# Four graph layers on one core: the attention blocks' biases added off TensorE, the first block's entry reordered, three buffers for the last mixing sets, the block loop written out

## The reference

```
h = relu(layernorm(x)); x = x + L0(h)    # 2 x [A_norm @ h @ W_gcn + b; leaky_relu(h @ W_mlp + b)]
h = relu(layernorm(x)); x = x + L1(h)    # 4 blocks, see below
h = relu(layernorm(x)); x = x + L2(h)    # h = x @ W + b, 3 diffusion steps with a 0/1 adjacency
h = relu(layernorm(x)); x = x + L3(h)    # 2 relational layers; w[r] = sum_b att[r, b] * basis[b]
```

```
y = cond_layer_norm(x, cond, s1, b1)
q, k, v = y @ wq + bq, y @ wk + bk, y @ wv + bv       # 4 heads of 128
x = x + (segment_softmax(q[src] . k[dst]) @ v) @ wo + bo
y = cond_layer_norm(x, cond, s2, b2)
x = x + relu(y @ m_w1 + m_b1) @ m_w2 + m_b2
```

## Time and profile before

| | |
|---|---|
| median of 3 runs | 886.33 us |
| profiled execution | 891.0 us, span 889.3 us |
| TensorE busy | 839.7 us, 94% |
| VectorE busy | 560.2 us, 63% |
| ScalarE busy | 398.0 us, 45% |
| GpSimd busy | 231.4 us, 26% |
| mean granted clock of TensorE | 0.985 |

### The profile page before, as it was taken

The page is one execution under the profiler, slowest core; times in us unless marked ns, Lnnn a source line. Parts: engine busy times, 40 slices in busy tenths (PEclk is TensorE's granted clock), DMA queues, the critical chain, the costliest instruction groups (busy, mean ns, idle before and its releaser), DMA issues. The chain is left out here.

```text
span 889.3 us, 13979 instructions
## 1 busy us (share of the span) xinstructions
PE 839.7 (94%) x4222; PEld 636.4 (72%) x4223; DVE 560.2 (63%) x1221; ACT 398.0 (45%) x646; POOL 231.4 (26%) x253
## 2 busy tenths in 40 slices
PE   4999789999889999999997999999999998999998
PEld 2666557667677778777695777787786965688786
DVE  5999987748957666576656476664776664730110
ACT  3999893325345612355322365223563233531210
POOL 5000023207422124402235122234013414412200
PEclk9999999999999999999999999999999998999999
DMA  7999914715525653636541546436477377220100
GB/s 167 192 214 241 275 39 124 188 58 133 154 59 123 179 125 107 147 102 178 122 136 54 140 98 183 100 106 146 102 193 176 115 192 184 56 96 0 48 13 35
DMA packets 37846, 113.39 MB, mean 128 GB/s; under 512 B 5908, under 2 KB 6472, under 8 KB 30108
## 3 DMA queue, kind: packets, MB, share of 16 engines
q1 hardware_dynamic: 20604, 79.00, 37.5%
q10 hardware_dynamic: 17184, 33.69, 11.3%
HBM read 105.33 MB, written 7.34 MB: 127 GB/s over the span
## 5 line engine op out<-in xcount | busy, mean ns | idle before, releaser
L690 POOL TENSOR_TENSOR wl<-wraw,wh 128x512 fp32r<-128x512 f32 x140 | 179.7, 1318 | 395.3 <-ACT wh L768 361.7
L1806 PE MATMUL ring<-ohs,ohd 128*128 128x512 f32 x312 | 80.2, 410 | 6.4 <-DVE ohs L1317 6.4
L1806 PEld LDWEIGHTS ring<-ohs,ohd 128*128 128x128 f32 x312 | 59.2, 195 | 31.5 <-issue 18.6
L1295 DVE SCALAR_TENSOR_TENSOR ohd<-iota,dstT,vals 128x256 fp32r x156 | 69.9, 481 | 9.2 <-PE ring L1806 5.6
L768 ACT ACTIVATE wh<-wraw 128x2048 fp32r<-128x2048 f32 x35 | 66.8, 1909 | 9.4 <-DMA wraw<-in_L_gnn_root 4.7
L793 ACT ACTIVATE yT_h<-ring 128x512 fp32r<-128x512 f32 x32 | 19.0, 598 | 98.7 <-PE ring L1722 98.7
L817 ACT ACTIVATE ohs<-iota,minus_srcT 128x512 fp32r<-128x512 f32 x78 | 52.4, 713 | 17.4 <-PE ring L1806 11.1
L1733 PE MATMUL mix_ps<-quad,att_shift 120*32 120x512 f32 x384 | 52.0, 622 | 3.7 <-DMA quad<-in_L_gnn_basis 3.7
L695 POOL TENSOR_TENSOR rstd<-ve,half 128x1 f32<-128x1 f32 x44 | 24.2, 553 | 111.9 <-DVE ve L1146 111.6
L1704 PE MATMUL ring<-yT_h,wh 128*128 128x512 f32 x128 | 49.8, 389 | 0.0
L1704 PE MATMUL ring<-yT_l,wh 128*128 128x512 f32 x128 | 49.8, 389 | 0.0
(11 more groups left out here) (390 smaller groups left out, 2157.4 us busy)
## 6 DMA issues: line engine op xcount, KB each, us to landing
quad<-in_L_gnn_basis SPq DMA_DIRECT2D x60, 960.0 KB, 8.2
wraw<-in_L_gnn_m_w ACTq DMA_DIRECT2D x8, 1024.0 KB, 6.0
mix_scratch<-mixed SPq DMA_DIRECT2D x128, 32.0 KB, 3.9
wraw<-in_L_gnn_wv ACTq DMA_DIRECT2D x4, 1024.0 KB, 5.3
wraw<-in_L_gnn_wq ACTq DMA_DIRECT2D x4, 1024.0 KB, 5.1
wraw<-in_L_gnn_wk ACTq DMA_DIRECT2D x4, 1024.0 KB, 5.3
wraw<-in_L_gnn_wo ACTq DMA_DIRECT2D x4, 1024.0 KB, 5.4
wraw<-mix_scratch ACTq DMA_DIRECT2D x4, 1024.0 KB, 5.7
```

Source lines behind the costliest of these rows:

```text
L690: last = g.tensor_tensor(wl[s][:, k, :], wraw[s][:, k, :], wh[s][:, k, :].bitcast(F32), ALU.subtract)
L1295: return v.scalar_tensor_tensor(out, at.unsqueeze(1).broadcast_to([P, 4, HALF]), dstT[:, e], vals[:, e, :].rearrange("p a b -> p (a b)").u ...
L1806: last = te.matmul(ring[:, banks[b], :], ohd[:, s, b, :], ohs[:, s, :], start=False, stop=False)
```

## The change

1. bv, bo and m_b2 are loaded as rows broadcast to 128 partitions. bv is added by VectorE as v leaves PSUM (into `vm_raw`, which shares its place with `vm_l`); ScalarE then makes the high part from SBUF and GpSimd the low part. bo and m_b2 are added to `xl` by GpSimd before the products o and X are added. m_b1 becomes a column: ScalarE applies it with the Relu, makes a shifted copy, and VectorE forms the low part from that. The bias products are gone.
2. At the entry, `tile_taken` for the last H tiles follows the maximum, the addition to x comes with the statistics, masks and adjacency casts move to just before block 0's first softmax, and the step weights to after the last head's transposed probabilities.
3. Sets 14 and 15 use all three buffers.
4. Blocks 1 and 2 are written out on every engine.

```diff
-COLUMN_BIASES = ("bq", "bk")
+COLUMN_BIASES = ("bq", "bk", "m_b1")
...
+        vm_raw = sb("vm_raw", [P, NT, D], ctx=unsplit_rows)
+        unsplit_rows.close()
         vm_l = sb("vm_l", [P, NT, D], F32R, ctx=c1)
...
             def load_group(t, k):
 
-                if not isinstance(t, int) or t >= EARLY_SETS:
+                late = (t - (SETS - 2)) * GROUPS + k if isinstance(t, int) else 0
+                if late >= 2:
+                    if late >= QSLOTS:
+                        sp.wait_ge(quad_used, (SETS - 2) * GROUPS + late - QSLOTS + 1)
+                elif not isinstance(t, int) or t >= EARLY_SETS:
                     sp.wait_ge(quad_used, t * GROUPS + (k - 1))
...
+            def load_value_bias(i):
+                sp.dma_start(value_bias[:], l1["bv"][bass.ds(i, 1)].broadcast_to([P, D])).then_inc(value_bias_loaded, 16)
+
+            def load_row_bias(name, i):
+                sp.dma_start(row_bias[:], l1[name][bass.ds(i, 1)].broadcast_to([P, D])).then_inc(row_bias_loaded, 16)
...
-            sp.wait_ge(tile_taken, n0.end)
+            sp.wait_ge(x_added, NT)
             sp.dma_start(rows(x_s), x[:]).then_inc(x_stored, 16)
...
                 load_group(t, 3)
+                sp.wait_ge(row_bias_added, i * (2 * NT) + NT)
+                load_row_bias("m_b2", i)
                 if not last:
-                    sp.wait_ge(brow_ready, i + 1)
-                    load_biases(nxt)
+                    sp.wait_ge(tile_taken, n1.base + i * PER + (n1.at[("v", NT - 1)] + 1))
+                    load_value_bias(nxt)
...
             def block_lows(i, last):
...
+                def add_row_bias(j, after):
+                    pool.wait_ge(row_bias_loaded, i * 32 + (16 * j + 16))
+                    pool.wait_ge(tile_taken, b + (T.at[after] + 1))
+                    for t in range(NT):
+                        g.tensor_tensor(xl[:, t, :], xl[:, t, :], row_bias[:], ALU.add).then_inc(row_bias_added, 1)
+
+                def low_values():
+                    for t in range(NT):
+                        pool.wait_ge(value_hi, i * NT + (t + 1))
+                        g.tensor_tensor(vm_l[:, t, :], vm_raw[:, t, :], vm_h[:, t, :].bitcast(F32), ALU.subtract
+                                        ).then_inc(value_split, 1)
+
+                for j in (1, 2):
+                    low_weight(i * 6 + (W1 + j), j % 3)
+                add_row_bias(0, ("Sa", NT - 1))
+                low_values()
+                for j in (3, 4):
                     low_weight(i * 6 + (W1 + j), j % 3)
                 for t in range(NT):
                     inverse_root(i * 8 + (12 + t), t)
-                for j in (5, 6):
-                    low_weight(i * 6 + (W1 + j), j % 3)
+                low_weight(i * 6 + (W1 + 5), 2)
+                add_row_bias(1, ("Sb", NT - 1))
+                low_weight(i * 6 + (W1 + 6), 0)
...
+                def values():
+                    for t in range(NT):
+                        act.wait_ge(tile_taken, after(("v", t)))
+                        a.activation(vm_h[:, t, :], vm_raw[:, t, :], ACT.Copy).then_inc(value_hi, 1)
+
+                def hidden(m):
+                    hi(("M", m), vm_h[:, m, :], ACT.Relu, bias=column_bias(2, m))
+                    act.wait_ge(hi_ready, i * PERH + (HI1 + hi_of[("M", m)] + 1))
+                    a.activation(vm_raw[:, m, :], vm_h[:, m, :].bitcast(F32), ACT.Identity,
+                                 bias=minus_hidden[:, bass.ds(i * KT + m, 1)]).then_inc(hidden_shifted, 1)
...
                 hwi(1)
-                value(0)
                 hwi(2)
-                value(1)
                 norm_rows("a", 2)
                 norm_rows("a", 3)
-                value(2)
                 query_key(0)
-                value(3)
+                values()
+                if first:
+                    neighbours()
...
             def first_layer_out(t):
-                leaky(1, t)
-                v.tensor_tensor(x[:, t, :], x[:, t, :], hv[:, t % 2, :], ALU.add).then_inc(tile_taken, 1)
+                dve.wait_ge(slope_ready, NT + t + 1)
+                v.tensor_tensor(hv[:, t % 2, :], bank(n0, ("H", 1, t)), slope[:, t % 2, :], ALU.max).then_inc(tile_taken, 1)
 
             def first_layer_stats(t):
                 taken(n0, n0.base, ("H", 1, t))
+                v.tensor_tensor(x[:, t, :], x[:, t, :], hv[:, t % 2, :], ALU.add).then_inc(x_added, 1)
+                dve.wait_ge(x_added, t + 1)
...
                 def value(t):
-                    lo(("v", t), vm_l[:, t, :], vm_h[:, t, :])
+                    ready(T, b, ("v", t))
+                    dve.wait_ge(value_bias_loaded, i * 16 + 16)
+                    v.tensor_tensor(vm_raw[:, t, :], bank(T, ("v", t)), value_bias[:], ALU.add).then_inc(tile_taken, 1)
+
+                def hidden(m):
+                    dve.wait_ge(hidden_shifted, i * KT + (m + 1))
+                    v.scalar_tensor_tensor(vm_l[:, m, :], bank(T, ("M", m)), minus_hidden[:, bass.ds(i * KT + m, 1)], vm_raw[:, m, :],
+                                           ALU.max, ALU.subtract).then_inc(tile_taken, 1)
 
                 def residual(name, t):
+                    dve.wait_ge(row_bias_added, i * (2 * NT) + ((0 if name == "o" else NT) + t + 1))
...
                 value(3)
 
+                if first:
+                    finish_masks()
+                    dve.wait_ge(mask_ready, NT)
                 masked(0)
...
                         done(("PT", h, m))
+                        if h == 0:
+                            pe.wait_ge(value_split, i * NT + (m + 1))
...
-            with pe.Fori(1, BLOCKS - 1) as i:
+            for i in range(1, BLOCKS - 1):
                 attention_block(i, False)
```

More of the change, by code:

```diff
@@ L945, in block_highs @@
                 T = n1_last if last else n1
+                hi_of = hi1_last if last else hi1
                 b = i * PER + n1.base
@@ L1033, in block_highs @@
                 for m in range(KT):
-                    hi(("M", m), vm_h[:, m, :], ACT.Relu)
+                    hidden(m)
                 if not last:
@@ L1044, in _ @@
             block_highs(0, False, True)
-            with act.Fori(1, BLOCKS - 1) as i:
+            for i in range(1, BLOCKS - 1):
                 block_highs(i, False)
@@ L1609, in attention_block @@
                 for m in range(KT):
-                    lo(("M", m), vm_l[:, m, :], vm_h[:, m, :], func=ALU.max, scalar=0.0)
+                    hidden(m)
                 split_cond(1, i * 2 + 3)
@@ L1972, in part, with rows_product @@
                     return ins
-                def rows_product(name, t, lh, ll, w, bias):
-                    tile((name, t), [bias_to_rows(bias, brow)] + [p for k in range(KT) for p in
-                         three(cols(lh, k, t), cols(ll, k, t), w[0][:, k, :], w[1][:, k, :])])
+                def rows_product(name, t, lh, ll, w):
+                    tile((name, t), [p for k in range(KT) for p in three(cols(lh, k, t), cols(ll, k, t), w[0][:, k, :], w[1][:, k, :])])
                 def columns_product(name, m, w, rh, rl):
@@ L1984, in value @@
                         done(("Ta", t))
-                    out = begin(T, b, ("v", t))
-                    part(out, [p for k in range(KT) for p in three(cols(yT_h, k, t), cols(yT_l, k, t), w[0][:, k, :], w[1][:, k, :])],
-                         first=True)
-                    if t == 0:
-                        pe.wait_ge(brow_ready, i + 1)
-                    part(out, [bias_to_rows(0, brow)], last=True).then_inc(tile_ready, 1)
+                    rows_product("v", t, yT_h, yT_l, w)
                 def query_key(h):
@@ L2071, in attention_block @@
                 outs[0] = begin(T, b, ("o", 0))
-                part(outs[0], [bias_to_rows(3, brow)] + head(0, 0) + head(0, 1), first=True)
+                part(outs[0], head(0, 0) + head(0, 1), first=True)
                 mix_in_block(1)
@@ L2075, in attention_block @@
                 outs[1] = begin(T, b, ("o", 1))
-                part(outs[1], [bias_to_rows(3, brow)] + head(1, 0) + head(1, 1), first=True)
+                part(outs[1], head(1, 0) + head(1, 1), first=True)
                 done(("PV", HEADS - 2))
@@ L2108, in attention_block @@
                     out = begin(T, b, ("X", t))
-                    part(out, [bias_to_rows(5, brow)], first=True)
                     for k in range(KT):
@@ L2112, in attention_block @@
                             done(("M", k))
-                        end = part(out, three(cols(vm_h, k, t), cols(vm_l, k, t), w[0][:, k, :], w[1][:, k, :]), last=k == KT - 1)
+                        end = part(out, three(cols(vm_h, k, t), cols(vm_l, k, t), w[0][:, k, :], w[1][:, k, :]), first=k == 0, last=k == KT - 1)
                     end.then_inc(tile_ready, 1)
```

98 lines of the change are left out of this document (52 added, 46 removed).

## The result

The changed kernel takes 876.44 us (median of 4 runs, 875.41 to 877.83), the kernel before in the same comparison 885.57: ratio 0.9876, 95% interval 0.985 to 0.9902. The two medians lie 9.1 us apart, and the ratio stands for 11.0 us; 14.5 were forecast. 872 was the number, and 876.4 lies inside the range of 861 to 880. The profiled execution took 877.83 us (span 876.1), 13.2 us less than that of before.

A forecast was written before the change was run, and what follows sets the result against it. TensorE, busy 94% of the span, was taken as the bound. Terms -7.0 - 6.6 - 10.2 + 3.3 + 1.0 + 5.0 = -14.5 us from 886.33 gave 871.8, forecast as 872; range 861 to 880.

The forecast's parts named there:

- Step 1: Block loop written out: VectorE's idle stretch before the second pass goes, 7.0 us gained, bounds 0 to 7.0.
- Step 2: Third buffer for the last two mixing sets: TensorE's stop and slow clock go, 6.6 us gained, bounds 3 to 6.6.
- Step 3 and 4: Four blocks: removing TensorE's bias products gains 10.2 us net; their replacement in M and X loses 3.3 us.
- the part of the rival that has it fall in X: Clock falls in X, at the end of blocks: 8 us lost instead of 3.3; part of a rival given 0.20.
- Step 5: GpSimd's row-bias additions and value subtractions, 15 us per block, lie in its gaps: cost 0 in blocks 1 to 3.
- Step 6: Entry loses 1 us at v(2); moved masks and casts ahead of block 0's first softmax lose 5 us.
- The six contended operations: Block 0: VectorE's condition cast, split and four masks beside four GpSimd subtractions, up to 5 us more.
- over 1 was the sign given: Expected sign in block 0: mask rows over 1 us beside GpSimd, with a stop ahead of the second head's scores.
- the rival in which the chains cost more: Clock falls in X (8 instead of 3.3), 7 at the softmax, 2 at the entry: 879 us, chance 0.20.

The follow-up runs named there:

- before_both: The kernel before with only VectorE's block loop written out and three buffers for the last two mixing sets: 875.16 us, ratio 0.9857.
- rolled_others: The changed kernel with the block loop rolled again on SyncE, GpSimd, ScalarE and TensorE, straight on VectorE only: 874.65 us, ratio 0.9841.
- rolled_vector: The changed kernel with blocks 1 and 2 again a loop on VectorE, straight code on the other engines: 881.85 us, ratio 0.9927.

## Why the prediction was nearly right

- *Step 1, the loop (-7.0).* Right in cause; alone it brought 9.8 us between the marks, 7.5 of them in block 2. The bound of 7.0 was too low: it took the first pass of the loop as the measure, which is itself 0.5 us longer than straight code, and left out the rest. Within this change the loop is worth 4.0.
- *Step 2, the buffers (-6.6).* 6.6 measured alone. Within this change it is worth 1.5 us. So neither this term nor that of step 1 can be added to the others without asking what those do to the same stop, and the split below holds for one order only: the two edits first, the others behind them.
- *Step 3 and 4, bias products less their chain (-10.2 + 3.3 = -6.9 over four blocks).* Against before_both, blocks 1, 2 and the rest gained 1.8, 1.8 and 3.0 us. In each of the two blocks 0.3 belongs to the other engines' loops (rolled_others), so the bias work has 1.5 + 1.5 + 3.0 = 6.0; with the same 1.5 in block 0, where it can't be read apart, 7.5. It was never run by itself. The mechanism was as described: X(0) waits 0.26 us for `vm_l` (0.5 foretold), Ta(0) 0.73, Ta(1) 0.42. The granted clock is 1.00 in blocks 1 and 2, so the part of the rival that has it fall in X is out. (3 x 0.9 + 0.5 is 3.2, not 3.3.)
- *Step 5, GpSimd's additions (0).* Right for the row additions: no wait of TensorE or of a residual names them. Not right for the value subtractions in block 0, whose price stands in step 6.
- *Step 6, entry and head 0 (+1.0 + 5.0).* This is the step that failed in size. Block 0 costs 134.18 against 123.86 us in before_both; with its bias gain of about 1.5, and less the 1.5 ahead of the marks, the loss is 11.8 - 1.5 = 10.3 us against 6.0. The entry's share: from the first transposes to v(2) 19.3 us instead of 15.5, 3.8 less 1.5 = 2.3 against 1.0, as the load of wk took 10.3 us; just outside the bound of 2.2. Head 0's share is what remains, 8.0 against 5, outside the bounds of 2 to 7. The six contended operations were named rightly and lost 3.1 us in all (the four masks took 3.59 us, 0.90 each, where over 1 was the sign given). What was missed is who stood behind them. The value tile is queued behind the condition split, ScalarE's casts behind the value tile, and the slower clock behind the stop. In this step the rival in which the chains cost more (7 and 2) was the nearer one.
- *The sum.* 15.0 us from the two edits against 13.6, 7.5 against 6.9 from the bias work, and 0.6 from the other engines' loops, which had no term, are 2.6 us more gained; 4.3 more were lost in step 6. The errors have opposite signs, which is luck, and left the sum 1.3 us off in the profiled executions (13.2 against 14.5; the start of H(1) gives 0.4 of it back). The medians lie 9 to 11 us apart, less than the profiled pair: the profiled execution of before was 4.7 us above the median of 886.33 and the one after 1.4 above its own. The prediction had noted the first and set the whole gain off against the median. Starts of H(1) between 211.4 and 215.7 us are of that size; that they are the cause was not shown for the unprofiled runs.

## What to carry to other kernels

Where a product moves from the bound engine to another, price the queue behind it there: the eight products of M (0.96 us a block) came back as a ScalarE pass (0.9), and two edits at the side, alone, gave at least as much as the whole change. A stop of a helper engine has no price of its own; it is worth what stands behind it, 3.1 or 7.5 us in the same block for the same loop, 1.5 or 6.6 for the same buffer. And read small effects between marks of the timeline, not between spans, when an early stage differs from run to run.

## What the hardware showed

- A VectorE cast of 128x1024 that takes 0.68 us alone took 1.74 when it began 0.1 us behind a GpSimd subtraction, and 4.79 when it began beside a GpSimd addition that three subtractions followed without a gap; four tiny values (`hasedge`) took 0.66 instead of 0.16. VectorE operations with an input in PSUM kept their time (value tiles 0.68, masked scores 0.69 us). The Trainium skill ("SBUF — State Buffer", SBUF: two separate sides) says that whichever of the two engines starts first holds the shared ports for a whole instruction. The 4.79 us are longer than one instruction: the cast ended 0.55 us behind the third subtraction.
- VectorE's loop over two blocks had an idle stretch of 5.22 us in rolled_vector and 5.76 in the kernel before, at the start of the second pass, where its one jump back is. The loops of the four other engines cost blocks 1 and 2 0.3 us each, together.
- TensorE's granted clock stayed at 1.00 (2.4 GHz) after a stop of 1.30 us and stood at 0.67 around one of 3.75; behind the stop of 3.02 us in the kernel before it was 0.51 from 248.70 to 252.00. After 4.12 and 5.84 us 16 transposes took 3.67 us, after 1.26 and 1.74 us 1.97.
